# Attention steps of a decoder kernel reordered on TensorE and ScalarE, with values computed by halves

## What is computed

```python
x = x + L0_attn(layernorm(x))                  # gated recurrence, no scores
x = x + L0_xattn(layernorm(x), ctx, ctx)       # 16 heads of 8, rotary, scores against ctx
x = x + L0_ffn(layernorm(x))                   # 16 routed and 2 shared experts
x = x + L1_attn(layernorm(x))                  # "long" attention over all tokens, and "short"
                                               # attention over tokens of the same segment
x = x + L1_xattn(layernorm(x), ctx, ctx, mask) # scores of 16 heads, masked ("given")
x = x + L1_ffn(layernorm(x))                   # 8 experts of width 512
# every attention: softmax(q k^T / sqrt(8) [masked]) v, per head
```

## Time and profile before

| | us |
|---|---|
| median of 3 runs | 525.63 (525.22 to 527.25) |
| profiled execution, its own time | 524.45 |
| its span, first to last instruction | 522.5 |
| outside the span | 1.95 |
| mean granted TensorE clock | 0.897 of 2.4 GHz |

### The profile page before, as it was taken

The page is one execution under the profiler, slowest core; times in us unless marked ns, Lnnn a source line. Parts: engine busy times, 40 slices in busy tenths (PEclk is TensorE's granted clock), DMA queues, the critical chain, the costliest instruction groups (busy, mean ns, idle before and its releaser), DMA issues.

```text
span 522.5 us, 13889 instructions
## 1 busy us (share of the span) xinstructions
PE 429.0 (82%) x5548; PEld 282.6 (54%) x5548; DVE 364.6 (70%) x889; ACT 264.5 (51%) x393; POOL 162.3 (31%) x296
## 2 busy tenths in 40 slices
PE   1865788877768999769888887788898769999996
PEld 1433466654335666435665665544544436767675
DVE  5573557773498888836886878657557446899995
ACT  1051345542435776426665656435334536687772
POOL 5204223120245788533333333132222300132110
PEclk9987559988698999956999999879979878999999
DMA  7000010000001114000000000000000001111201
GB/s 254 0 1 1 10 57 3 3 2 1 0 16 33 59 45 151 1 0 3 3 3 2 3 3 3 1 13 12 23 1 3 3 0 42 43 42 48 74 1 41
DMA packets 9065, 13.08 MB, mean 25 GB/s; under 512 B 1450, under 2 KB 7474, under 8 KB 9010
## 3 DMA queue, kind: packets, MB, share of 16 engines
q1 hardware_dynamic: 9012, 12.32, 7.6%
HBM read 11.79 MB, written 0.52 MB: 24 GB/s over the span
## 4 chain that ended last, share of the span: by engine, by line
PE 34%; DVE 16%; ACT 3%; POOL 2%; issue 2%; DVEq 0%; POOLq 0%
DVE smax L1306 7%; PE bk L901 3%; PE sc L1142 3%; PE sc L1144 3%; PE sc L1143 3%; PE bk L1167 3%; PE bk L1157 3%; PE bk L1159 3%; PE sc L845 3%; DVE inv_sum L1321 2%; PE sc L834 1%; PE bk L894 1%; PE bk L877 1%; PE sc L832 1%; PE bk L944 1%
## 5 line engine op out<-in xcount | busy, mean ns | idle before, releaser
L1306 DVE TENSOR_REDUCE smax<-sc 128x8 f32<-128x1024 f32 x64 | 78.0, 1220 | 59.0 <-PE sc L845 59.0
L615 ACT ACTIVATE probs<-sc 128x1024 f32<-128x1024 f32 x64 | 65.3, 1024 | 65.6 <-PE sc L845 65.5
L1547 DVE SCALAR_TENSOR_TENSOR x_all<-bk,comb,x_all 128x128 f32<-128x128 f32 x208 | 58.1, 343 | 1.7 <-PE bk L1167 1.3
L534 POOL TENSOR_TENSOR gated_lo<-gated,gated_hi 128x512 f16<-128x512 f32 x36 | 41.7, 1158 | 33.4 <-ACT gated_hi L689 33.4
L720 ACT ACTIVATE probs<-sc,w 128x512 f32<-128x512 f32 x64 | 40.7, 686 | 15.0 <-PE sc L1144 15.0
L894 PE MATMUL bk<-probs,v_pad 128*32 128x128 f32 x1024 | 40.9, 306 | 8.2 <-ACT probs L615 4.4
L440 POOL TENSOR_TENSOR w_lo<-w,w_hi 128x1024 f16<-128x1024 f32 x8 | 18.0, 2250 | 74.1 <-ACT w_hi L607 74.1
L1653 DVE TENSOR_TENSOR p_lo<-probs,p_hi 128x1024 f16<-128x1024 f32 x32 | 38.4, 1223 | 3.6 <-ACT p_hi L727 3.0
L894 PEld LDWEIGHTS bk<-probs,v_pad 128*32 128x32 f32 x1024 | 29.9, 121 | 15.8 <-issue 13.2
L1321 DVE RECIPROCAL inv_sum<-bk 128x128 f32<-128x128 f32 x32 | 30.3, 948 | 11.1 <-PE bk L901 11.1
L689 ACT ACTIVATE gated_hi<-gated 128x512 f16<-128x512 f32 x36 | 22.7, 630 | 29.6 <-DVE gated L1535 29.6
(11 more groups left out here) (247 smaller groups left out, 1061.6 us busy)
## 6 DMA issues: line engine op xcount, KB each, us to landing
w<-in_w SPq DMA_DIRECT2D x8, 514.0 KB, 4.0
w<-in_w SPq DMA_DIRECT2D x18, 192.0 KB, 2.4
wd<-in_wd SPq DMA_DIRECT2D x1, 644.0 KB
x_all<-in_x SPq DMA_DIRECT2D x1, 512.0 KB, 4.1
ctxT<-in_ctx_t SPq DMA_DIRECT2D x4, 128.0 KB, 3.3
ctx_tok<-in_ctx SPq DMA_DIRECT2D x4, 128.0 KB, 2.2
mask_in<-in_mask SPq DMA_DIRECT2D x4, 128.0 KB, 2.7
out<-x_all SPq DMA_DIRECT2D x1, 512.0 KB, 3.2
```

Of the source, the lines that this page charges most:

```text
L534: pool.tensor_tensor(gated_lo[:, k % DEPTH, :], gated[:, k % DEPTH, :], gated_hi[:, k % DEPTH, :], ALU.subtract).then_inc(c_glo, 1)
L615: act.activation(probs[:, n % 2, half, :], sc[half][:, :], ACT.Exp, scale=HD ** -0.5).then_inc(u_exp, 1)
L1306: dve.tensor_reduce(smax[:, s, 8 * half:8 * half + 8], sc[half][:, :].rearrange("p (h k) -> p h k", k=S), X, ALU.max).then_inc(u_max, 1)
L1547: op = dve.scalar_tensor_tensor(x_all[:, bb, :], (bk4, bk5)[k % 2][:, b * 128:(b + 1) * 128], w, x_all[:, bb, :], ALU.mult, ALU.add)
```

## The change

- **Stacks.** `q_stack` and `k_stack` have four buffers instead of two (in the memory of `p_hi`); POOL's split waits for the maxima's transposes of four members back. Layernormed x has separate slots by pair (`slot_of`), the mask's bfloat16 form has three buffers instead of two.
- **TensorE's order.** The maxima's transposes of a member move from between its predecessor's numerators and sums to after S(0) of the next member (before it where r is given or absent). Then come the projections of the next pair, then T(1) and T(0) together, then the stack transposes, then S(1). Projections of values (cross) and of segment logits (long) become functions of their own, behind S(1).
- **Values by halves.** Numerators and sums become `values`: 16 numerator matmuls and 16 sums of half 1 after its exponential, then the same for half 0. Between them, in the second half-step, stand the output projections of q.
- **ScalarE's order.** The copies of maxima's transposes and of projections come before the two exponentials; in step 13 the copy of the last maxima's transposes stands behind the weights' split.
- **VectorE and POOL.** The sum of the rotary parts, the tests and products for tokens alone in their segment (`alone`) and the mask's bfloat16 form move from VectorE to POOL. The layernorm statistics of `nxt` move from the end of the step to behind the first member's maxima, but only where there is no `late`; with `late` (steps 4, 6, 8, 10) they stay at the end.
- **SyncE.** Masks are loaded ahead of ctx, each with its own wait.

The diff's core, for POOL (stacks, split, `stage`), ScalarE (`stage`), TensorE (`values`, and its whole `stage` as it stands after the change) and VectorE (`stage`), in this order:

```diff
-        q_stack = sb("q_stack", [128, 2, H * SLOT], F16)
-        k_stack = sb("k_stack", [128, 2, H * SLOT], F16)
+        q_stack, k_stack = (p_hi[:, k, :, :].rearrange("p h (n c) -> p (h n) c", c=H * SLOT) for k in range(2))
...
             def split_high(p, s):
                 if p.kind == "cross":
+                    pool.wait_ge(rope_rd, n + 1)
+                    pool.tensor_tensor(qkv[:, s, 0:2 * D], rope_c[:, s, :], rope_s[:, s, :], ALU.add).then_inc(rope_m, 1)
                     pool.wait_ge(rope_m, n + 1)
...
-                if n >= 2:
-                    back = 2 if p.kind == "cross" or p.kind == "given" and p.i or n < UNITS_D + 2 else 4
-                    pool.wait_ge(u_qm_ps, n - back + 1)
+                if n >= 4:
+                    pool.wait_ge(u_qm_ps, n - 3)
...
             def stage(r, p, q, nxt=None, late=None, ahead=None, last=None):
                 if p:
                     copy_values(p, 0)
+                if r and r.kind == "given":
+                    inputs_given(r)
                 if r:
                     ...
                     split_high(r, 0)
                     split_low(r, 0)
+                if nxt and not late:
+                    finish_norm(nxt)
                 if p:
                     copy_values(p, 1)
...
             def stage(r, p, q, nxt=None, late=None, ahead=None, last=None):
+                own = r and r.kind in ("long", "segment")
                 if q:
-                    exp(q.n + 1, 1)
+                    stacks_m(q.n + 1, 1)
+                if own:
+                    inputs(r, 0)
+                if q:
+                    exp(q.n + 1, 1)
                     exp(q.n + 1, 0)
...
                     stacks(p.n + 1, 1)
+                    stacks_m(p.n, 0)
+                if own:
+                    inputs(r, 1)
+                if p:
                     exp(p.n, 1)
                     exp(p.n, 0)
...
-                if p:
-                    stacks_m(p.n + 1, 1)
                 if ahead:
                     evac_parts(ahead, 0)
                 if ahead == LN_F:
                     weights1_high(0, 1, 0)
                     weights1_high(1, 1, 1)
...
+            def values(n, s, half):
+                own_v = lambda g, at: v_pad[:, s, g, at:at + 32]
+                own_one = lambda g, at: ones_pad[:, at:at + 32]
+                if half == 1:
+                    pe.wait_ge(u_vpad, n + 1)
+                    if n >= 1:
+                        pe.wait_ge(u_norm, n)
+                pe.wait_ge(u_exp, 2 * n + 2 - half)
+                products(s, half, AV, own_v)
+                mm = products(s, half, SUMS, own_one)
+                if half == 0:
+                    mm.then_inc(u_av, 1)
...
             def stage(r, p, q, nxt=None, late=None, ahead=None, last=None):
                 plain = not r or r.kind == "given"
                 if q and plain:
                     stack_maxima(q, 1, p)
                 if p:
                     scores(p, 0, 0)
                 if r and r.kind in ("cross", "long"):
                     normed(r)
                 if q and not plain:
                     stack_maxima(q, 1, p)
                 if not plain:
                     inputs(r, 0, q)
                 if q:
                     scores_T(q, 1, 1, p)
                     scores_T(q, 1, 0, p)
                 if p:
                     stack_T(p, 1)
                 if late:
                     late_transposes(late)
                 if p:
                     scores(p, 0, 1)
                 if r and r.kind == "cross":
                     values_of(r, 0, q)
                 if r and r.kind == "segment":
                     segments(r)
                 if q:
                     values(q.n + 1, 1, 1)
                     values(q.n + 1, 1, 0)
                 if late:
                     late_fusion(late)

                 if p and plain:
                     stack_maxima(p, 0, True)
                 if p:
                     scores(p, 1, 0)
                 if p and not plain:
                     stack_maxima(p, 0, True)
                 if not plain:
                     inputs(r, 1, q)
                 if p:
                     scores_T(p, 0, 1, True)
                     scores_T(p, 0, 0, True)
                 if r:
                     stack_T(r, 0)
                 if p:
                     scores(p, 1, 1)
                 if r and r.kind == "cross":
                     values_of(r, 1, q)
                 if r and r.kind == "long":
                     logits_of_segments(r)
                 if p:
                     values(p.n, 0, 1)
                 if q and q.kind == "segment":
                     late_projections(q, r)
                 elif q and q.kind != "long":
                     outputs(q, r)
                 if p:
                     values(p.n, 0, 0)
...
             def stage(r, p, q, nxt=None, late=None, ahead=None, last=None):
                 if q:
                     normalise(q, 0)
+                if r and r.kind == "cross":
+                    rotate(r, 0)
                 if p:
                     maxima(p, 0, 1)
                 ...
+                if nxt and not late:
+                    start_norm(nxt)
```

More of the change, by code:

```diff
@@ L282, in slot_of @@
         def slot_of(p):
[L284 removed]
+            return (4 if p.kind == "given" else 0) + 2 * (p.i % 2)
         def place(n):
@@ L516, in stage @@
                     weights1_low(1, 1)
-                if nxt:
-                    at = slot_of(nxt)
-                    rsqrt((LN_B if nxt.kind == "cross" else LN_D) + nxt.norm, 2, at=at)
-                    if nxt.kind == "given":
-                        pool.wait_ge(e_any, 3 * nxt.i + 3)
-                        pool.tensor_tensor(rstd_any[:, at:at + 2], rstd[:, at:at + 2], mask_any[:, :, 1], ALU.mult)\
-                            .then_inc(e_q, 1)
+                if nxt and late:
+                    finish_norm(nxt)
                 if r:
@@ L526, in stage @@
                     split_low(r, 1)
+                if r and r.kind == "segment":
+                    alone(r)
             rsqrt(LN_B, 2)
@@ L855, in scores @@
                     pe.wait_ge(e_mask, p.i + 1)
+                if half == 0 and n >= 1:
+                    pe.wait_ge(u_max, 2 * n - 1)
                 if half == 0 and n >= 2:
@@ L962, in segments, with outputs @@
                 mm.then_inc(d_cnt_ps, 1)
-            def outputs(q):
+            def outputs(q, r):
                 pe.wait_ge(u_norm, q.n + 2)
+                if r and r.kind == "cross":
+                    pe.wait_ge(v_sb, r.n + 2)
                 if q.kind == "given":
@@ L1048, in stage @@
                 if p:
-                    scores_T(p, 0, 0, True)
                     scores(p, 1, 1)
-                if r:
-                    inputs(r, 1, q)
+                if r and r.kind == "cross":
+                    values_of(r, 1, q)
+                if r and r.kind == "long":
+                    logits_of_segments(r)
+                if p:
+                    values(p.n, 0, 1)
                 if q and q.kind == "segment":
@@ L1461, in stage @@
                     normalise(q, 1)
+                if r and r.kind == "cross":
+                    rotate(r, 1)
                 if p:
```

266 lines of the change are left out of this document (129 added, 137 removed).

## The result

The changed kernel takes 525.89 us, median of 20 runs (520.80 to 529.73); before takes 523.36 us, median of 20 (517.44 to 527.98), 2.3 under the median of three from which the forecast was taken. The ratio is 1.0077, 95% interval 1.0046 to 1.0108: 0.8% slower, where 514.5 us was forecast. Ratios leave out executions more than 1.5% above the fastest of their kernel, which the medians given here keep (one of e4 took 580.5 us at a mean clock of 0.722); without them the changed kernel's median is 525.10, and differences to it are up to 0.8 us smaller.

The account below looks back on a forecast made before the run. No engine was full; TensorE was nearest, at 85% in steady steps, with holes ended by the loop of scores and maxima. Terms -4.1 + 1.0 - 2.0 - 7.0 + 1.0 = -11.1 us, from 525.63 to 514.5 us, range 504 to 524.

Parts of the forecast that it names:

- Starts (-4.1): Start of both loops: second member's projections run during POOL's first split; 4.1 us less, between -6 and -1.5.
- Steady steps (+1.0): Cross, long and segment steps: extra matmul groups and exponential waits slightly outweigh removed holes; 1.0 us more, pair 27.6 us.
- Without r (-2.0): Steps 4 and 5 of the first loop, 12 and 13 of the second: shorter half-steps, 2.0 us less.
- Masked steps (-7.0): Steps 8 to 12: 78.0 us in place of 85.0, 7.0 us less, between -9.5 and -4.
- End (+1.0): Step 13: last maxima's copy waits behind the weights' split on ScalarE; 1.0 us more, between 0 and +2.
- Rival 4: 20 half-steps with projections: S(1) and values wait for the exponential of half 1, 0.75 us each; 529.5 us, chance 0.10.
- Rival 5: Values in 10 steps: each break in the stream of like matmuls costs some 0.3 us; 517.5 us, chance 0.05.

Follow-up runs that it names:

- e4: Changed kernel with the rotary sum and the lone tokens' tests and products back on VectorE; 521.43 us, ratio to before 0.9979.
- e7: e2 with the start of both loops as before: first member's stack transposes ahead of the second's projections; 520.46 us, ratio to before 0.9991.
- e2: Changed kernel with TensorE's and ScalarE's old order and layernorm statistics at the step's end in long and segment steps; 514.18 us, ratio to before 0.9819.
- e13: Changed kernel with POOL's reciprocal root of the next layernorm moved behind its second copy of the values; 516.70 us, ratio to before 0.9897.
- e10: Changed kernel with ScalarE's copies of the projections behind the exponential of half 1 in long and segment steps; 513.46 us, ratio to before 0.9884.
- e9: e8 with the order of before also in the four steps with given inputs; 509.91 us, ratio to before 0.9815.
- e8: e2 with ScalarE's weights' split of the next stage behind the last exponentials; 511.85 us, ratio to before 0.9837.
- e1: Changed kernel with TensorE's and ScalarE's order of before in long and segment steps; 515.94 us, ratio to before 0.9875.
- e3: Changed kernel with statistics, masks' tests and reciprocal root at the step's end in every step; 533.89 us, ratio to before 1.0203.
- e5: Changed kernel with the stack transposes issued twice in long and segment steps, filling TensorE's hole before S(1); 524.97 us, ratio to before 1.0071.

## Why the prediction was wrong

- **Starts (-4.1): right in kind, too small.** 4.5 us earlier at the second loop's projections in the profiled execution, 6.3 by the medians of e7 and e2. I had not counted that a shorter start also moves the clock's rise: the first loop's first step has clock 0.67 in e2 and 0.52 in e7. The sum of the rotary parts, which I put at 0.6 us on POOL, took 0.72.
- **Steady steps (+1.0): here it failed.** Not the size of what I counted: with POOL's root out of the way a pair takes 27.54 us, where I had 27.6, holes of 0.4 to 0.7 where I had 0.7 to 0.9. The failed step is "POOL is busy 9.04 of 27.30 us, which hides it", and "where the layernorm moves to the middle it delays the next maximum by 0.45". I asked how busy POOL is, and what the statistics delay on VectorE. I did not ask what stands behind the moved root on POOL's own queue: the copy of the values, and behind that the copy on ScalarE and the exponential. I had priced that copy at its length, 0.2 us more hole, and not looked at what it waits for: POOL stood 2.80 us for the statistics, the copy 1.28 us for POOL, and the hole became 1.10 us. Cost: 0.7 us a pair, and by way of the clock most of the rest of 9.2 us (e13).
- **The clock.** I held it at 2.4 GHz in the steady steps because it was 1.00 before. In the changed kernel it fell in steps 3 and 7. Twice (1 minus the clock) times the span is an estimate of the time at 1.2 GHz: 105 us in the changed kernel (median of its runs), 86 in e13, 83 in e10. Of the 9.2 us that e13 gained, three pairs explain 2.1; the 19 us fewer at half the clock allow up to 9. So most of the loss against e13 was the clock's, and I had it in no term. Against the kernel before it is no loss in sum: that one has 101 to 105 us too (medians of its runs beside the experiments). What the starts and the masked steps saved of low clock, steps 3 and 7 took back.
- **Without r (-2.0): wrong.** Step 4 takes 14.51 us for 13.90 at clock 0.78 for 0.88, and the first loop's last outputs are added 4.2 us earlier than before though that step began 7.2 earlier. It is not that TensorE idles more there (2.81 us of it for 3.90): each half-step of mine assumed full clock. The terms of my half-step add to 4.8 us, not to the 5.3 that I wrote, so by them the term would have been -3.0, farther off.
- **Masked steps (-7.0): right in sum**, 6.4, by step 14.16, 17.23, 15.46, 17.67, 14.13 against 12.3, 18.3, 15.6, 17.6, 14.2. In part that is luck: step 8 missed by +1.9 and step 9 by -1.1. Step 8's miss is not the clock's, since e13 takes the same 15.23 us for it at 1.00 as the changed kernel at 0.89 (from maximum to maximum). T(0) of step 11 waited 2.97 us for the maximum, where I had 3, that of step 9 only 1.91. The order was not the reason for the gain (e9).
- **End (+1.0): right in sign.** TensorE stood 3.33 us for the copy behind the weights' split; step 13 took 10.8 us for 10.2; moving the split gave 2.3 by the medians (e8).
- **The rivals.** Rival 4, "the exponential uncovered", is what happened, by the queue that I named and with ScalarE's copies in front, but not by its price of 0.75 us in each of 20 half-steps: in the long and segment steps 0.7 in every fourth, and the clock. Rival 5 is not borne out: e10 has the breaks that it names, and its pair is as long as that of e1. The Trainium skill, "TensorEngine Tiling (Array Packing)", Key Properties, has each change of tiling mode drain TensorE. By the prediction's count both orders change mode as often in a step, so the equal pairs (27.14 and 27.12 us) agree with it and give no price for a drain.

What makes the clock fall stays open. The longest hole does not decide it. Before the change TensorE had holes of up to 1.08 us in the steady steps, and more idle time in a pair (4.05 us for 2.95), at clock 1.00:

```profile
258.73 0.34 PE L845 MATMUL sc<-qmT,qkT 32*128 32x128 f16 x6 [1.08 <-DVE smax L1306]
```

e13 has the hole of 1.04 us in step 7 (316.07) too, e10 one of 1.12 there (312.37), e3 one of 1.27 in a steady pair (310.26), each at clock 1.00. Step 5 of the changed kernel has the hole of 1.10 and keeps the clock. That the wait let through by POOL and ScalarE leads to the low clock is shown by e10 and e13; by which property of the holes is not.

e13 is nearer to the kernel that I had costed: one move on POOL, and its steady pair is 27.54 us for the 27.6 of the sum. But its 516.70 us are 6.8 under the 523.5 of before beside it, where the sum had 11.1. The 4.3 that are left may lie in the steps without r (-2.0, not seen) and the end; no run places them.

## What to carry to other kernels

Before moving an instruction onto an in-order queue, write down what stands behind it there and follow that across engines until it reaches the bound: the queue's busy share says nothing on it. An instruction in front of a critical one costs its wait, not its length. And give the clock a term of its own: here a wait of 0.7 us a pair went with some 7 us more from low clock, which no count of its own microseconds would have shown.

## What the runs showed of the hardware

TensorE's clock fell in steady steps after holes of 1.10 us at most: step 2, 10.80 of 12.51 us busy, and the first part of step 3 went before the first fall. In e5 the same holes filled in part kept it up in step 3, and the fall came in steps 7 and 8. No hole length marks the fall: holes of 1.08 (before), 1.12 (e10) and 1.27 us (e3) left the clock at 1.00. The Trainium skill, "TensorE: Matmul & The Clock Gate", A second HAM failure mode: psum-queue depth-cycling, describes such a thing: frequent short idles between groups of matmuls make the clock go up and down. This trace agrees in that no single hole in these steps is longer than 1.10 us; the trace of before, with more idle time in its steady steps and clock 1.00, shows that short idles alone do not bring it about. The 20 runs of the kernel before scatter by 2% (517.4 to 528.0), so a difference under 1% could be told only from medians of many runs.
